# Head attention on one core: the low part of the summed rows made by TensorE and ScalarE, and the probabilities scaled by VectorE

## The reference, cut to what matters

```python
Q = (x @ Wq).reshape(N, H, D)          # N = 6250 nodes, H = 8 heads of D = 32
K = (x @ Wk).reshape(N, H, D)
V = (x @ Wv).reshape(N, H, D)
score = jnp.einsum('nhd,ngd->nhg', Q, K) / np.sqrt(D)
score = jax.nn.softmax(score, axis=-1)
x1 = jnp.einsum('nhg,ngd->nhd', score, V).reshape(N, H * D)
src, dst = (edge_index[0], edge_index[1])
msg = x1[dst] * x1[src]
attn_out = jax.ops.segment_sum(msg, dst, num_segments=N)
...
```

## Time and profile before

| | us |
|---|---|
| time, median of 3 runs (2807.16 to 2810.66) | 2809.49 |
| span of the profiled execution | 2807.3 |
| `attention_rows` in it: first transpose at 50.3, last summed row at 362.8 | 312.5 |
| one turn of its loop of 8 tiles, 146.88 to 194.10 | 47.22 |
| the same per tile | 5.90 |
| DVE busy over the span | 2163.7 (77%) |
| PE busy over the span | 2557.3 (91%) |
| POOL busy over the span | 519.6 (19%) |

### The profile page before, as it was taken

The page is one execution under the profiler, slowest core; times in us unless marked ns, Lnnn a source line. Parts: engine busy times, 40 slices in busy tenths (PEclk is TensorE's granted clock), DMA queues, the critical chain, the costliest instruction groups (busy, mean ns, idle before and its releaser), DMA issues. The chain is left out here.

```text
span 2807.3 us, 47621 instructions
## 1 busy us (share of the span) xinstructions
PE 2557.3 (91%) x15898; PEld 2077.0 (74%) x15898; DVE 2163.7 (77%) x3416; ACT 1268.5 (45%) x2040; POOL 519.6 (19%) x615
## 2 busy tenths in 40 slices
PE   3999979999999999968888888869999999999996
PEld 2666657777777777745555555539999999999996
DVE  6999867777777777746666656659998988989896
ACT  1233257777777777723223332235433333333332
POOL 2999920000000000011222212200000000000000
PEclk9999999999999999989999999989999999999998
DMA  3111012222222222240122102136545545454543
GB/s 99 42 45 44 33 71 106 100 99 99 99 99 99 99 99 99 107 169 27 40 66 66 66 3 63 40 90 138 117 93 112 119 83 119 85 117 89 119 88 72
DMA packets 404977, 240.05 MB, mean 86 GB/s; under 512 B 325024, under 2 KB 396576, under 8 KB 398560
## 3 DMA queue, kind: packets, MB, share of 16 engines
q1 hardware_dynamic: 383968, 215.50, 27.9%
q10 hardware_dynamic: 19824, 19.32, 2.1%
q0 software_dynamic: 1040, 3.41, 0.4%
HBM read 48.65 MB, written 110.84 MB: 57 GB/s over the span
## 5 line engine op out<-in xcount | busy, mean ns | idle before, releaser
L1755 PE MATMUL d_acc<-d_rows_high,d_weights_high 128*128 128x258 f32 x2401 | 685.9, 286 | 19.0 <-DVE d_weights_low L1621 13.2
L1756 PE MATMUL d_acc<-d_rows_low,d_weights_high 128*128 128x258 f32 x2401 | 679.8, 283 | 0.0
L1757 PE MATMUL d_acc<-d_rows_high,d_weights_low 128*128 128x258 f32 x2401 | 679.1, 283 | 0.0
L1378 PE MATMUL b_pagg<-x_parts,b_counts 128*128 128x512 f32 x2401 | 653.2, 408 | 0.3 <-ACT b_counts L1421 0.3
L1695 ACT CAST d_weights_high<-d_weights 128x896 fp32r<-128x896 f32 x343 | 322.3, 945 | 533.8 <-PE d_acc L1757 276.7
L1378 PEld LDWEIGHTS b_pagg<-x_parts,b_counts 128*128 128x128 f32 x2401 | 422.9, 189 | 72.7 <-ACT b_counts L1421 0.9
L1755 PEld LDWEIGHTS d_acc<-d_rows_high,d_weights_high 128*128 128x128 f32 x2401 | 455.8, 190 | 27.5 <-DVE d_weights_low L1621 16.8
L1756 PEld LDWEIGHTS d_acc<-d_rows_low,d_weights_high 128*128 128x128 f32 x2401 | 456.1, 190 | 2.2 <-issue 2.2
L1757 PEld LDWEIGHTS d_acc<-d_rows_high,d_weights_low 128*128 128x128 f32 x2401 | 456.2, 190 | 0.0
L1621 DVE TENSOR_TENSOR d_weights_low<-d_weights,d_weights_high 128x896 fp32r<-128x896 f32 x343 | 372.6, 1086 | 68.9 <-ACT d_weights_high L1695 68.7
L1420 ACT CAST b_counts<-b_pcounts 128x784 fp32r<-128x784 f32 x392 | 319.9, 816 | 222.8 <-PE b_pcounts L1391 222.8
(11 more groups left out here) (158 smaller groups left out, 2679.9 us busy)
## 6 DMA issues: line engine op xcount, KB each, us to landing
edge_counts<-b_counts SPq DMA_DIRECT2D x49, 1568.0 KB, 5.2
node_table<-u_table ACTq DMA_DIRECT2D x7, 903.0 KB, 9.7
qx<-in_x SPq DMA_DIRECT2D x49, 128.0 KB, 2.0
x_table<-x_tile ACTq DMA_DIRECT2D x49, 128.0 KB, 1.7
agg<-b_sums SPq DMA_DIRECT2D x49, 128.0 KB, 4.6
u_x<-x_table SPq DMA_DIRECT2D x7, 896.0 KB, 9.6
u_agg<-agg SPq DMA_DIRECT2D x7, 896.0 KB, 11.4
u_x<-in_x SPq DMA_DIRECT2D x7, 896.0 KB, 4.9
```

The lines of the kernel that those rows point to most:

```text
L1378: last = nc.tensor.matmul(pagg[:, o, :], ca[:, o, hi, :], x1_parts[:, hi].rearrange("p m d -> p (m d)"), start=(hi == 0), stop=(hi == TILE ...
L1755: nc.tensor.matmul(acc[:, r, 0:HT], a, high[:, t, :], start=(t == 0), stop=False)
L1756: nc.tensor.matmul(acc[:, r, 0:HT], a, low[:, t, :], start=False, stop=False)
L1757: last = nc.tensor.matmul(acc[:, r, 0:HT], b, high[:, t, :], start=False, stop=(t == TILES - 1))
```

## The change

PE gets one product more per tile. At step T, between the products for tile T-1 and the sum over heads for tile T-4, it multiplies the high part of tile T-6 with an identity matrix times -1 and lets it accumulate onto the sums that still stand in `x1_sum`; what is left there is the low part. ACT copies that out, as its second job of the step, before the exponential, and signals `low`. DVE's subtraction for the low part (L397) is gone. The scaling of the exponentials moves from POOL (L337) to DVE, where it stands between the maximum and its subtraction; POOL then begins with the product with V. A wait of the sum (L371) on `probs` is gone too, since both are now DVE's. PE and ACT have 6 steps of delay instead of 4 and 5, DVE 2 instead of 5. The slot rule for the sums, `free(pe, low, t, 2)`, is unchanged, so the sum over heads for tile T-4 still waits until the low part of tile T-6 is out.

```diff
+        minus = sb("minus_ident", [P, P], F32R)
...
@@ tensor, between the products for T-1 and the sum for T-4
+                    t, s = T - 6, u % 2
+                    if is_tile(t):
+                        if isinstance(T, int) and t == 0:
+                            pe.wait_ge(minus_ready, 1)
+                        pe.wait_ge(high, T - 5)
+                        nc.tensor.matmul(x1_sum[:, s:s + 1, 0:D], minus[:], part(0, t), start=False, stop=True,
+                                         skip_group_check=True).then_inc(less_high, 1)
                     t, s = T - 4, u % 2
...
@@ scalar, between the copy for T and the exponential for T-2
+                    t, s = T - 6, u % 2
+                    if is_tile(t):
+                        act.wait_ge(less_high, T - 5)
+                        nc.scalar.copy(part(1, t), x1_sum[:, s:s + 1, 0:D]).then_inc(low, 1)
...
@@ gpsimd
-                        pool.wait_ge(inverted, T - 1)
-                        nc.gpsimd.tensor_tensor(sc[:, q], sc[:, q], rs[:, q % 2].unsqueeze(2).broadcast_to([P, N_HEADS, N_HEADS]),
-                                                ALU.mult).then_inc(probs, 1)
...
@@ vector
-                        free(dve, probs, b, 2)
...
+                    if is_tile(b):
+                        dve.wait_ge(inverted, T - 1)
+                        nc.vector.tensor_tensor(sc[:, qb], sc[:, qb], rs[:, qb % 2].unsqueeze(2).broadcast_to([P, N_HEADS, N_HEADS]),
+                                                ALU.mult).then_inc(probs, 1)
...
-                    t, s = T - 5, (u - 1) % 2
-                    if is_tile(t):
-                        dve.wait_ge(high, T - 4)
-                        nc.vector.tensor_tensor(part(1, t), x1_sum[:, s:s + 1, 0:D], part(0, t), ALU.subtract).then_inc(low, 1)
+
+                nc.vector.tensor_scalar(minus[:], c["ident"][:], -1.0, None, ALU.mult).then_inc(minus_ready, 1)
```

More of the change, by code:

```diff
@@ L226, in attention_rows @@
         high, low = kit.sem("x1_high"), kit.sem("x1_low")
+        minus_ready, less_high = kit.sem("minus_ident_ready"), kit.sem("x1_less_high")
         def is_tile(t):
@@ L290, in step @@
                         last.then_inc(x1_summed, 1)
-                tile_steps(pe, step, 4)
+                tile_steps(pe, step, 6)
             @block.scalar
@@ L325, in step @@
                         act.dma_start(x1_out[rows(t), :], x1[:, q, :]).then_inc(x1_stored[q], 16)
-                tile_steps(act, step, 5)
+                tile_steps(act, step, 6)
                 for n in range(QUAD):
@@ L393, in step @@
                                                 ALU.subtract).then_inc(shifted, 1)
-                    t, s = T - 5, (u - 1) % 2
-                    if is_tile(t):
-                        dve.wait_ge(high, T - 4)
-                        nc.vector.tensor_tensor(part(1, t), x1_sum[:, s:s + 1, 0:D], part(0, t), ALU.subtract).then_inc(low, 1)
-                tile_steps(dve, step, 5)
+                nc.vector.tensor_scalar(minus[:], c["ident"][:], -1.0, None, ALU.mult).then_inc(minus_ready, 1)
+                tile_steps(dve, step, 2)
 def group_steps(eng, body):
```

## The result

The changed kernel takes 2829.89 us (median of 6 runs, 2828.32 to 2830.35) against 2808.96 of the kernel before in the same rounds: 20.9 us more. The ratio is 1.0067, with a 95% interval of 1.0048 to 1.0085, which is 13 to 24 us. The forecast was 2834.7 us in a range of 2822 to 2852.

The account below looks back on a forecast made before the run. PE was to set the pace through its round trip to ACT: +23.7 us for 42 steps, +1.0 turns, +1.1 last K, -0.6 POOL, sum +25.2. That gives 2832.5 from the profiled span; forecast 2834.7 us, range 2822 to 2852.

Parts of the forecast that it names:

- one round trip per tile on PE: Before PE's sum over heads: new product, ACT's copy and both hand-overs lie on PE in full, once per tile.
- The size of the step: PE's new step in the attention loop, start to start: 6.48 us, from 6.22 with low ends to 6.81 with high ends.
- to the end of the new product: On PE from the transposition: 2.89 us (2.81 to 2.96) to the new product, then 0.28 (at most 0.38) for it.
- to ACT: From the new product's end to ACT's copy: hand-over 0.10 us (0.05 to 0.11) plus register step 0.05 (0 to 0.1).
- back to PE: From the end of ACT's low-part copy to the start of PE's sum over heads: 0.10 us, between 0.05 and 0.16.
- from the sum to the transposition: On PE, from the sum over heads to the next tile's transposition: 2.68 us, between 2.66 and 2.70.
- The turns of the loop: Register steps of the engines at each turn of the loop: 0.2 us for each of five turns, +1.0 together.
- The stage's end: After step 48: +1.1 us because K of the last tile comes later, -0.6 for two scalings lost by POOL.
- DVE's short ring: DVE's step, then exponential and copy of K on ACT: 5.72 us per tile plus 0.1 for the scaling, at most 5.98.
- Hidden round trip: Rival: low part is out before PE reaches the sum, short ring decides; 2800.7 to 2811.6 us, chance 0.08.
- The clock: Rival: PE's longer idle time lowers its clock; one step in five at 1.2 GHz gives 2862 us, chance 0.06.
- That DVE and POOL meet: Rival: scaling contends with POOL over SBUF; 0.6 more gives 2838 us, a hold for POOL's whole product 126 more; chance 0.03.

Follow-up runs that it names:

- e2: Changed kernel with the scaling back on POOL, low part still by product and copy: 23.7 us over the kernel before, ratio 1.0086.
- e3: Changed kernel with the new product issued first in PE's step, ahead of the transposition: 3.7 us under the kernel before, ratio 0.9986.
- e4: Changed kernel with ACT's copy of K put ahead of its copy of the low part: 2832.7 us, ratio 1.0085 to the kernel before.
- e9: Changed kernel with ACT copying the sums once more, into a spare tile, before the low part's copy: 2839.6 us, ratio 1.0109 to the kernel before.
- e5: e3 with the copy of K also put ahead of the exponential on ACT: 2794.57 us, 14.2 under the kernel before, ratio 0.9955.
- e1: Kernel before with only the scaling moved from POOL to DVE, which still makes the low part: 2.0 us under the kernel before, ratio 0.9993.
- e7: Changed kernel with one more small DVE product per tile, both operands in SBUF, during POOL's product: 2951.8 us (one run).
- e8: Changed kernel with one more small DVE product per tile, one operand in PSUM, during POOL's product: 25.3 us over the kernel before (one run).
- e6: Kernel before with the copy of K put ahead of the exponential on ACT: 2807.5 us, ratio 0.9995 to the kernel before.

## Why the prediction was right, point by point

**The bound and the new wait.** Right: one round trip per tile on PE, released by the copy of the low part. The foretold signs were a spacing of 6.4 to 6.5 (6.39 came), about 0.6 us of PE idle before the sum (0.64), DVE's wait for K over 1 us (1.24), POOL's wait for the scaling about 1.4 (1.29), the scaling at 0.22 (215 ns) and a clock of 1.00, and all came or came close. e2, e3, e4 and e9 show that the wait carries the loss and that all of it lies on PE.

**The size of the step.** 6.48 was forecast, 6.39 came, and the sum for the program was 25.2 us where 20.9 was measured. Measured terms, in the order of the prediction: to the end of the new product 3.08 (183.09 - 180.01) where I had 2.89 + 0.28 = 3.17; to ACT 0.12 where I had 0.10 + 0.05; the copy 0.37 (0.38); back to PE 0.15 (0.10); from the sum to the transposition 2.67 (2.68). The mis-sized term is the first, and in it the start of the new product. I took half of the 0.15 that lay before L288 as PE's own, and all of it was wait: in e5 the sum starts 2.80 after the transposition (183.04 to 185.84), which is the low end of my range, and 2.80 + 0.28 is the 3.08. Counted from the end of the products with Wv, the new one ends 0.11 later (182.98 to 183.09). The Trainium skill, TensorE: Matmul & The Clock Gate, section "Step-by-step: what each phase is for", says that in a stream the drain of one product overlaps the fill of the next. The trace agrees, with 0.11 for 256 columns. Those two ends are modelled, but ACT's starts say the same: what the products with Wv release starts 3.00 after the transposition (e4, 206.80 to 209.80), what the new product releases without a register step starts 3.12 after it (e9, 208.93 to 212.05).

The hand-over to ACT came out close (0.12 for 0.15) because two errors cancel in part: 0.10 was taken for the bare hand-over and 0.05 for the register step, and measured were 0.03 to 0.04 and 0.08 to 0.09.

**The rest of the sum.** Of the 5.6 us between 25.2 and the 19.55 of the profile, the loop makes 5.0: 42 steps were 19.7 and not 23.7 + 1.0. The turns of the loop were priced at 0.2 each and cost 0.03 (6.41 against 6.38); in e3 and e5, where PE doesn't wait for ACT, a turn costs 0.3. That PE's wait covers them is my reading of this and not shown by a run of its own. The 0.6 ahead of step 6 had no term at all. The stage's end was priced at +1.1 - 0.6 = +0.5 and came out as -0.8. K of the last tile was 0.9 later, and with two scalings gone from POOL the last sum over heads starts 0.4 later than before, counted from the last transposition. Behind its end 0.5 more pass until the next stage starts, in which the last tile's product by minus one and its copy stand; they had been taken as hidden. But the sum itself ran in 2.86 instead of 4.54 us, which is 1.7 less and had no term either. The granted clock over it was 1.00 in the changed kernel and 0.62 in the kernel before; PE had been idle for 0.60 and 2.61 us ahead of it. In the two stretches below, of the changed kernel and then of the kernel before, the clock is the last figure but two; 1.00 is the 2.4 GHz level, and 0.62 is a mean between the two levels:

```profile
377.80:380.70 2.90, 2.85 (x13) 2.39 (x13) 0.00 (x0) 0.41 (x2) 0.00 (x0) 1.00 0.13 45
```

```profile
357.10:361.65 4.55, 4.54 (x12) 3.37 (x12) 0.00 (x0) 0.00 (x0) 0.00 (x0) 0.62 0.00 0
```

**The scaling.** 0.1 was taken for DVE's short ring between 0 and 0.26; the subtraction starts 0.27 after the maximum instead of 0.26. It was next to nothing, and e1 shows no cost in the time either.

**The rivals.** Hidden round trip: not so, but e3 is that case made real. It was priced at 2800.7 to 2811.6, and e3 took 2805.5. The clock did not fall in the loop. That DVE and POOL meet: the argument that POOL has nothing to do while the scaling runs holds inside the loop, where the scaling lasts 215 ns; it failed in one step of 49, the last, where no tile is left to keep the order, and there it was covered. That rival had two prices. The one read from the update stage (0.57) doesn't hold here; the other, 126 us if DVE is held for a whole product of POOL, is near what e7 cost.

## What to carry to other kernels

When work moves from one engine to two, ask what stands directly behind the first half on its own queue: if that waits for the second half, the hand-over there and back lies on the engine, however idle the helper is. The cure took no more work here: the first half is issued as early in the step as its inputs allow, so that the engine has its own work to do while the helper answers. Then look for the next ring: e3 alone gained 3.7 us on the kernel before, and 14.2 came only when the copy of K was moved too (e5). And before an instruction is moved from GpSimd to VectorE, look where its operands lie and what GpSimd runs at that time.

## What the runs showed of the hardware

- A VectorE instruction with both operands in SBUF that starts while a GpSimd product runs ends with it: 3.24 us instead of 0.2 (e7), 3.01 at the end of the changed kernel. With one operand in PSUM it isn't held: 0.23 (e8).
- A register step between a wait and the instruction that it guards lies in the hand-over: ACT started the same copy 0.12 us after PE's end with it and 0.04 without (loop and unrolled steps of the changed kernel), and another copy 0.03 after it (e9). The step's own row lasts only 0.05.
- A product of 256 columns that stands in the trace as one row of 0.47 us adds 0.11 us behind the products with Wv (changed kernel) and 0.06 between the sum and the transposition (e5 against e6's short steps).
- A wait costs PE more than its idle time: 0.64 idle, 0.88 in the step (changed kernel against e5).
- The times of e2 and of the changed kernel differ by 3 us in their medians with stages that end 0.5 us apart. For differences of a few us the end of the stage in the profile says more here than the time of the program.
